# A graph layer's edge loop: who makes the turned selection matrix

## The chip, the cores and the metric

One Trainium2 chip, of which the kernel uses one core. The time is that of one execution on the device, in microseconds (us), as the median of several runs. A core has five engines that run their own instruction streams: PE (matrix multiply), DVE (vector), ACT (scalar, activations), POOL (GpSimd) and SP (DMA issue and semaphores). They meet by semaphores alone. Small differences, of about 0.3% (13 us here), can't be told from no change.

## The reference, cut to what matters

The layer works on N = 6250 nodes of 256 features and on E = 200000 edges (`src`, `dst`, sorted by `dst`). It adds a graph attention layer and a global polynomial attention ("mix"), and then a mixture of 16 experts. The change is in the edge part:

```python
xw = (x @ W).reshape(N, H, C)                 # H = 8 heads of C = 32
e = leaky_relu(a_src[src] + a_dst[dst], 0.2)  # one logit per edge and head
ex = exp(e - m[dst])
denom = segment_sum(ex, dst)
out = segment_sum(xw[src] * ex, dst) / denom  # then bias and relu
```

## The kernel before

The program goes through stages one after the other: setup and projections (to about 600 us of the profile), the edge loop (about 600 to 3510 us), routing (to about 3760 us), experts (to about 4220 us) and the last norm. Only the edge loop and two small allocations are touched.

The edge loop has 392 chunks of 512 edges (four tiles of 128). The edges are sorted by destination, and destinations lie in 49 blocks of 128 nodes, so a chunk on the border of two blocks is worked on twice: 440 steps, each with one chunk and one block. Over the first 208 steps the loop also computes the mix attention for 13 groups of 512 queries, one group in 16 steps (`query`, with k = 0 to 15 saying which pieces come in which step); the last 224 steps have edge work only. Here is who does what in step s:

- POOL gathers the 128 rows of each tile from `node_rows` by an indirect DMA (L923), four for a chunk, into a ring of R = 4 chunks (`rows_g`). Before it refills a slot it waits for `msg_ready`, that is, until DVE has finished (L1112) with the last step that needed the old chunk. SP counts the chunks that have landed (L940) and fetches the next indices (L936).
- ACT loads `dst_all[s+4]`, the chunk's destinations broadcast over 128 partitions (L962), computes `exp` of the logits into `msg` (L1010), and squares the mix features (L975), whose matmuls wait for it.
- DVE makes the two selections for step s+1. `sel_t` (L1030) has a node of the block in each partition and an edge in each column, and is 1 where the edge's destination is the node. It is made as `is_equal` of `dst_all` and the partition's number `iota_col`, in bf16. `sel` (L1036) has edges in the partitions and nodes in the columns, in fp32. Then it waits for the chunk (L1097) and for the spread values (L1098), and computes the logits (L1102, L1104, L1106), the block's sum of step s-2 (`accumulate`, L1045), a piece of the mix, and, after ACT's exp, the weighted rows (L1112).
- PE multiplies `sel_t` with the block's attention terms (`spread`, L1134, twelve small matmuls), which gives each edge its destination's terms; it waits for the logits of step s before it spreads for s+1. It multiplies `sel` with `msg` (`aggregate`, L1143, eight records). In the step order of PE, aggregate(s-1) comes first, then the mix pieces of the step, then spread(s+1).

There are two buffers of `sel_t`, so the one of step s may be overwritten when spread(s-2) is done (`dst_spread`). Four PSUM banks serve the mix pieces in turn, so that every fifth matmul waits until ACT or DVE has emptied the bank used four pieces earlier (`bank_free`, L885). `load_dst` in ACT's body waits for `sel_t_ready` of step s (L1011), because the loaded buffer is the one that `sel_t` of step s was made from.

Of the kernel before, what the change touches and what calls it, by code (L numbers as in the profile page):

```python
# [123 lines left out]
def gps_layer(nc, x, src, dst, gnn_W, att_src, att_dst, gnn_bias, Wqkv, bqkv, Wproj, bproj, temperature,  # L124
# [12 lines left out]
    with top:  # L137
# [14 lines left out]
        iota_col = sb("iota_col", [P, 1])  # L152
        ones = sb("ones", [P, P])
# [31 lines left out]
        blk_row = sb("blk_row", [1, SP_], I32, ctx=early)  # L185
        need_row = sb("need_row", [1, SP_], I32, ctx=early)
        first_row = sb("first_row", [1, CHUNKS], I32, ctx=early)
# [13 lines left out]
        with ExitStack() as c:  # L201
# [104 lines left out]
            def _(dve):  # L306
# [11 lines left out]
                dve.tensor_copy(iota_col[:], iota_ci[:])  # L318
                dve.wait_ge(ident_ready, 1)
# [352 lines left out]
        with ExitStack() as c:  # L672
# [58 lines left out]
            def _(dve):  # L731
# [21 lines left out]
                dve.tensor_copy(first_row[:], fdf[:])  # L753
# [21 lines left out]
                dve.tensor_scalar(blk_row[:], p_b[0:1, :], float(T - 1), None, ALU.min)  # L775
                dve.tensor_copy(need_row[:], p_need[0:1, :])
# [37 lines left out]
        with ExitStack() as c:  # L814
            idx = [sb(f"idx{i}", [P, TC], I32, ctx=c) for i in range(R)]
            rows_g = sb("rows_g", [P, R, TC, ROW], ctx=c)
            msg = [sb(f"msg{i}", [P, TC, ROW], ctx=c) for i in range(2)]
            dst_all = [sb(f"dst_all{i}", [P, TC * P], BF16, ctx=c) for i in range(R)]
# [136 lines left out]
            def _(act):  # L955
# [7 lines left out]

                def take_queries(n, g):
                    act.wait_ge(act_filled, act_count(n, f"T{g}"))
                    act.copy(q_t[g][:], bank(f"T{g}")[:]).then_inc(act_freed, 1)
# [39 lines left out]
                def body(s, k, n, last):  # L1006
                    j = k % R
                    wait(act, msg_summed, s - 1)
                    act.wait_ge(logit_ready, s + 1)
                    act.activation(msg[j % 2][:, :, D:ROW], lg[j % 2][:], ACT.Exp).then_inc(weight_ready, 1)  # L1010
                    act.wait_ge(sel_t_ready, s + 1)  # L1011
                    load_dst(s + R, j)
                    if n is not None:
                        query(n, k)

                load(0)
                for j in range(R):
                    load_dst(j, j)
                rounds(act, body)
# [5 lines left out]
            def _(dve):  # L1025
                def select_turned(s, j):

                    dve.wait_ge(dst_in[j], (s - j) * (16 // R) + 16)
                    wait(dve, dst_spread, s - 1)
                    dve.tensor_scalar(sel_t[j % 2][:], dst_all[j][:], iota_col[:], None, ALU.is_equal).then_inc(sel_t_ready, 1)  # L1030

# [56 lines left out]
                def body(s, k, n, last):  # L1088
# [6 lines left out]
                    select_turned(s + 1, j1)  # L1095
# [18 lines left out]
                select_turned(0, 0)  # L1114
# [731 lines left out]
```

## Time and profile before

| what | us |
|---|---|
| median of three runs | 4401.64 |
| lowest and highest | 4396.38, 4409.33 |
| the profiled execution, whole | 4418.26 |
| its span, first to last instruction | 4416.5 |

The profile is one execution. A row of its fifth part or of the view of groups names line, engine, operation and tiles, the count, the busy time and mean duration in ns of one, and then the idle time of the engine just before them with what ended it. In a timeline row the first number is the start, the second the duration, and the bracket tells how long the engine had been idle and who released it. A releaser is inferred; "issue" means that the profile shows nothing that was waited for, and "remote" that the release came from something that it can't name.

### The profile page before, as it was taken

The numbers are of one execution on the slowest core, as the hardware profiler recorded it, in microseconds if no ns is written. First come the engines' busy times: TensorE is split into PE (matmuls) and PEld (weight loads), VectorE is DVE, ScalarE is ACT, GpSimd is POOL, SyncE is SP. The second block draws the span as 40 slices with busy tenths as digits, with TensorE's granted clock in tenths as the row PEclk, the third lists the DMA queues.
The fourth block names the chain that finished last, engine by engine and source line by source line (L and its number), as shares of the span: only waits on it lengthen the run. The fifth ranks groups of instructions, "written<-read, shape, count | busy, mean of one in ns | idle before, by whom it ended". The sixth has DMA issues, their size and how long they took to land. (4 is left out here: it accounts for less than half of the span.)

```text
span 4416.5 us, 65073 instructions
## 1 busy us (share of the span) xinstructions
PE 2861.2 (65%) x15683; PEld 1908.1 (43%) x15684; DVE 2359.4 (53%) x5089; ACT 649.8 (15%) x1729; POOL 2272.4 (51%) x2161
## 2 busy tenths in 40 slices
PE   5888747777777777777554555555545542899940
PEld 2444324444444444444343333334334341788830
DVE  6888755544555554555554545545545674211137
ACT  2333212211221222222000000000000000122210
POOL 3777635554555555555566656656566555000035
PEclk9999868877878888888777777777777655999975
DMA  3000033333333333333333333433333312777743
GB/s 117 29 29 27 22 82 92 93 93 86 90 92 91 94 91 88 93 91 91 99 100 99 100 99 99 104 99 101 98 98 103 83 47 108 225 232 232 232 126 117
DMA packets 335340, 451.54 MB, mean 102 GB/s; under 512 B 113998, under 2 KB 247660, under 8 KB 335190
## 3 DMA queue, kind: packets, MB, share of 16 engines
q0 software_dynamic: 91088, 256.16, 21.0%
q1 hardware_dynamic: 172806, 128.68, 9.9%
q10 hardware_dynamic: 71328, 65.57, 5.5%
q14 instruction: 97, 0.79, 0.1%
q8 instruction: 21, 0.34, 0.0%
HBM read 395.09 MB, written 56.69 MB: 102 GB/s over the span
## 5 line engine op out<-in xcount | busy, mean ns | idle before, releaser
L923 POOL DMA_INDIRECT rows_g<-node_rows,idx x1568 | 1655.2, 1056 | 1284.2 <-DVE msg L1112 776.8
L1143 PE MATMUL p_m<-msg,sel 128*128 128x264 f32 x3520 | 1185.9, 491 | 255.1 <-DVE msg L1112 140.6
L1143 PEld LDWEIGHTS p_m<-msg,sel 128*128 128x128 f32 x3520 | 805.2, 241 | 438.7 <-issue 286.6
L1102 DVE TENSOR_TENSOR lg<-rows_g,p_m 128x32 f32<-128x32 f32 x440 | 81.5, 185 | 1116.0 <-remote 735.9
L1134 PE MATMUL p_m<-adm_parts,sel_t 128*128 x5292 | 247.0, 173 | 587.6 <-DVE lg L1106 469.9
L1134 PEld LDWEIGHTS p_m<-adm_parts,sel_t 128*128 128x128 bf16 x5292 | 216.1, 100 | 833.1 <-issue 808.3
L1112 DVE TENSOR_TENSOR msg<-rows_g,msg 128x1024 f32<-128x1024 f32 x440 | 540.7, 1229 | 24.2 <-ACT msg L1010 5.9
L1010 ACT ACTIVATE msg<-lg 128x32 f32<-128x32 f32 x440 | 101.2, 230 | 2001.2 <-DVE lg L1106 1476.3
L1036 DVE TENSOR_TENSOR sel<-iota_bf,dst_t 128x512 f32<-128x512 bf16 x441 | 301.0, 683 | 0.1
L975 ACT ACTIVATE qfeat<-p_scr 128x512 f32<-128x512 f32 x442 | 235.0, 601 | 440.1 <-remote 199.7
L1728 POOL DMA_DIRECT2D slot_y<-ysb x64 | 34.6, 541 | 472.9 <-DVE ysb L1718 472.9
L1030 DVE TENSOR_SCALAR sel_t<-dst_all,iota_col 128x512 bf16<-128x512 bf16 x441 | 168.3, 382 | 190.1 <-issue 175.8
L401 DVE TENSOR_TENSOR acc<-kk 128x512 f32<-128x512 f32 x250 | 251.3, 1037 | 0.1
L1671 PE MATMUL e_ph<-xst,wa 128*128 128x256 f32 x1024 | 234.1, 382 | 4.0 <-DMA bb<-in_L_ffn_b_dram 3.1
L1680 PE MATMUL e_py<-wb,ht 128*128 128x256 f32 x1024 | 231.4, 379 | 0.0
L1160 PE MATMUL p_scr<-q_t,sel_sum 32*128 32x512 f32 x832 | 187.7, 721 | 39.6 <-ACT qfeat L975 16.8
L401 POOL TENSOR_TENSOR acc<-kk 128x512 f32<-128x512 f32 x150 | 213.3, 1448 | 0.0
L1671 PEld LDWEIGHTS e_ph<-xst,wa 128*128 128x128 f32 x1024 | 196.1, 192 | 31.6 <-DMA bb<-in_L_ffn_b_dram 3.5
L1680 PEld LDWEIGHTS e_py<-wb,ht 128*128 128x128 f32 x1024 | 189.7, 190 | 23.2
L1045 DVE TENSOR_TENSOR acc<-acc,p_m 128x264 f32 x440 | 188.9, 429 | 4.4 <-PE p_m L1134 1.5
L1701 ACT ACTIVATE ht<-e_ph,ba 128x256 f32<-128x256 f32 x256 | 100.3, 474 | 422.5 <-PE e_ph L1671 422.5
L1710 DVE COPY xst<-e_px 128x512 f32<-128x512 f32 x64 | 44.3, 692 | 212.1 <-PE e_px L1661 212.1
(307 smaller groups left out, 3046.7 us busy)
## 6 DMA issues: line engine op xcount, KB each, us to landing
dst_all<-dst_bc ACTq DMA_DIRECT2D x444, 128.0 KB
wa<-in_L_ffn_w_dram SPq DMA_DIRECT2D x64, 512.0 KB, 3.9
wb<-in_L_ffn_w_dram SPq DMA_DIRECT2D x64, 512.0 KB, 5.2
rows_g<-node_rows,idx POOLq DMA_INDIRECT x1568
xs<-slot_x SPq DMA_DIRECT2D x64, 256.0 KB, 3.2
slot_y<-ysb POOLq DMA_DIRECT2D x64, 256.0 KB, 4.4
bb<-in_L_ffn_b_dram SPq DMA_DIRECT2D x64, 128.0 KB, 5.2
qs<-qn_dram ACTq DMA_DIRECT2D x14, 512.0 KB
```

The costliest lines, as they stand in the source:

```text
L401: return eng.tensor_tensor(feat.rearrange("p (d i) -> p d i", i=C), bass.AP(base.tensor, base.offset, [whole, [0, DIAGS - 1], [1, C]]), ba ...
L923: pool.indirect_dma_start(rows_g[:, j, u, :], None, node_rows, bass.IndirectOffsetOnAxis(ap=idx[j][:, u:u + 1], axis=0)).then_inc(gathered ...
L975: act.activation(feat[slot(name)][:], bank(name)[:], ACT.Square).then_inc(act_freed, 1)
L1030: dve.tensor_scalar(sel_t[j % 2][:], dst_all[j][:], iota_col[:], None, ALU.is_equal).then_inc(sel_t_ready, 1)
L1036: dve.tensor_tensor(sel[j][:], iota_bf[:].unsqueeze(1).broadcast_to([P, TC, P]), d.unsqueeze(2).broadcast_to([P, TC, P]), ALU.is_equal).th ...
L1045: dve.tensor_tensor(a, a, p_m[j % 2][:, 0:ROW], ALU.add).then_inc(acc_added, 1)
L1112: dve.tensor_tensor(m4, g3[:, :, 0:D].rearrange("p u (h e) -> p u h e", h=H), msg[j % 2][:, :, D:ROW].unsqueeze(3).broadcast_to([P, TC, H, ...
L1134: mm = pe.matmul(p_e(j)[:, u * 2 * H:(u + 1) * 2 * H], sel_t[j % 2][:, u * P:(u + 1) * P], adm_parts[:, bass.ds(b, 1), part, :].rearrange( ...
L1143: mm = pe.matmul(p_m[j % 2][:, 0:ROW], sel[j][:, u, :], msg[j % 2][:, u, :], start=(u == 0), stop=(u == TC - 1))
L1160: pe.matmul(bank(name)[:], sel_sum[rows, m * P:(m + 1) * P], q_t[g][rows, :], start=True, stop=True).then_inc(act_filled, 1)
L1671: mm = pe.matmul(p_h[s % 2][:, m * SLOT_ROWS:(m + 1) * SLOT_ROWS], wa[s][:, k, m * P:(m + 1) * P], xst[s % 2][:, k, :], start=(k == 0), st ...
L1680: mm = pe.matmul(p_y[s % 2][:, a * D:(a + 1) * D], ht[s % 2][:, k, a * P:(a + 1) * P], wb[s][:, k, :], start=(k == 0), stop=(k == KF - 1))
```

## The change

The turned selection `sel_t` is made by ACT in place of DVE. ACT takes the square of `dst_all - partition number` into a new bf16 tile `apart`, and then `relu(1 - apart)`, which is 1 where the difference is zero and 0 where it is another whole number. It does so for step s+2 in step s, after its exp and its load, ahead of the squares of the mix. The wait for `sel_t_ready` in ACT goes. DVE keeps `sel`. To find room for `apart`, three one-row tables share one tile (rows 0, 32 and 64 of it), which changes where they are read from and nothing else. One [128, 1] operation in the setup makes the negated partition number.

```diff
@@ setup
+        iota_neg = sb("iota_neg", [P, 1])
-        blk_row = sb("blk_row", [1, SP_], I32, ctx=early)
-        need_row = sb("need_row", [1, SP_], I32, ctx=early)
-        first_row = sb("first_row", [1, CHUNKS], I32, ctx=early)
+        tables = sb("tables", [2 * C + 1, SP_], I32, ctx=early)
+        blk_row = tables[0:1, :]
+        need_row = tables[C:C + 1, :]
+        first_row = tables[2 * C:2 * C + 1, 0:CHUNKS]
+                dve.tensor_scalar(iota_neg[:], iota_ci[:], -1.0, None, ALU.mult)
@@ edge loop
+            apart = [sb(f"apart{i}", [P, TC * P], BF16, ctx=c) for i in range(2)]
@@ scalar
+                def select_turned(s, j):
+
+                    act.wait_ge(dst_in[j], (s - j) * (16 // R) + 16)
+                    act.activation(apart[j % 2][:], dst_all[j][:], ACT.Square, bias=iota_neg[:])
+                    act.drain()
+                    wait(act, dst_spread, s - 1)
+                    act.activation(sel_t[j % 2][:], apart[j % 2][:], ACT.Relu, bias=ones[:, 0:1], scale=-1.0).then_inc(sel_t_ready, 1)
@@ scalar, body
                     act.activation(msg[j % 2][:, :, D:ROW], lg[j % 2][:], ACT.Exp).then_inc(weight_ready, 1)
-                    act.wait_ge(sel_t_ready, s + 1)
                     load_dst(s + R, j)
+                    select_turned(s + 2, (j + 2) % R)
                     if n is not None:
                         query(n, k)
@@ scalar, before the loop
+                for j in range(2):
+                    select_turned(j, j)
@@ vector
-                def select_turned(s, j):
-
-                    dve.wait_ge(dst_in[j], (s - j) * (16 // R) + 16)
-                    wait(dve, dst_spread, s - 1)
-                    dve.tensor_scalar(sel_t[j % 2][:], dst_all[j][:], iota_col[:], None, ALU.is_equal).then_inc(sel_t_ready, 1)
@@ vector, body
-                    select_turned(s + 1, j1)
                     select(s + 1, j1)
@@ vector, before the loop
-                select_turned(0, 0)
```

## Rows read from the trace of the kernel before

**Rows 1.** The page: each engine's busy time, share of the span, and count.
```profile
PE 2861.2 (65%) x15683; PEld 1908.1 (43%) x15684; DVE 2359.4 (53%) x5089; ACT 649.8 (15%) x1729; POOL 2272.4 (51%) x2161
```
**Rows 2.** Windows, edge loop with and without mix: busy (count) PE PEld DVE ACT POOL, clock.
```profile
604.00:2152.00 1548.00, 1153.15 (x6560) 651.98 (x6560) 811.28 (x1642) 315.03 (x711) 802.83 (x778) 0.82 0.35 92
2152.00:3515.00 1363.00, 734.23 (x4468) 539.67 (x4468) 704.08 (x1565) 51.44 (x224) 846.62 (x785) 0.73 0.38 100
```
**Rows 3.** Waits: engine and line, releaser, total us, times, longest.
```profile
POOL rows_g L923 <- DVE msg L1112: 776.8, 134, 11.8
...
DVE lg L1102 <- remote: 735.9, 135, 17.9
...
DVE lg L1102 <- SPq L940: 212.0, 30, 9.3
```
**Rows 4.** The page's groups, the gather and DVE's big operations in the edge loop.
```profile
L923 POOL DMA_INDIRECT rows_g<-node_rows,idx x1568 | 1655.2, 1056 | 1284.2 <-DVE msg L1112 776.8
...
L1036 DVE TENSOR_TENSOR sel<-iota_bf,dst_t 128x512 f32<-128x512 bf16 x441 | 301.0, 683 | 0.1
...
L1030 DVE TENSOR_SCALAR sel_t<-dst_all,iota_col 128x512 bf16<-128x512 bf16 x441 | 168.3, 382 | 190.1 <-issue 175.8
```
**Rows 5.** Timeline from 2823 us, a burst without mix work.
```profile
2823.20 0.19 DVE L1102 TENSOR_TENSOR lg<-rows_g,p_m 128x32 f32<-128x32 f32 x1 [9.73 <-remote]
...
2824.37 1.22 DVE L1112 TENSOR_TENSOR msg<-rows_g,msg 128x1024 f32<-128x1024 f32 x1
2825.70 3.86 PE L1143 MATMUL p_m<-msg,sel 128*128 128x264 f32 x8 [0.86 <-DVE msg L1112]
...
2826.43 1.32 POOL L923 DMA_INDIRECT rows_g<-node_rows,idx  x1 [5.90 <-DVE msg L1112]
2826.85 0.18 DVE L1102 TENSOR_TENSOR lg<-rows_g,p_m 128x32 f32<-128x32 f32 x1
...
2831.17 0.19 DVE L1102 TENSOR_TENSOR lg<-rows_g,p_m 128x32 f32<-128x32 f32 x1 [0.21 <-issue]
```
**Rows 6.** Timeline of POOL: the gather that begins the next train.
```profile
2847.50 1.21 POOL L923 DMA_INDIRECT rows_g<-node_rows,idx  x1 [5.38 <-DVE msg L1112]
```
**Rows 7.** Timeline: first and last `sel_t` inside a gather pause, with the gather that ends it.
```profile
652.11 0.34 DVE L1030 TENSOR_SCALAR sel_t<-dst_all,iota_col 128x512 bf16<-128x512 bf16 x1
...
653.10 0.94 POOL L923 DMA_INDIRECT rows_g<-node_rows,idx  x1 [4.48 <-DVE msg L1112]
...
3478.77 0.35 DVE L1030 TENSOR_SCALAR sel_t<-dst_all,iota_col 128x512 bf16<-128x512 bf16 x1 [0.42 <-issue]
...
3479.24 1.29 POOL L923 DMA_INDIRECT rows_g<-node_rows,idx  x1 [4.51 <-DVE msg L1112]
```
**Rows 8.** Timeline of POOL: first and last gather that start while L1036 runs.
```profile
600.17 1.23 POOL L923 DMA_INDIRECT rows_g<-node_rows,idx  x1 [0.30 <-issue]
...
3500.72 1.23 POOL L923 DMA_INDIRECT rows_g<-node_rows,idx  x1 [0.30 <-issue]
```
**Rows 9.** Groups: ACT on 128x512, without and with a bias column; a table load.
```profile
L975 ACT ACTIVATE qfeat<-p_scr 128x512 f32<-128x512 f32 x442 | 235.0, 601 | 440.1 <-remote 199.7 <-PE p_scr L1160 117.7 <-PE p_scr L1173 68.9
...
L970 ACT ACTIVATE r_norm<-p_scr,c_col 128x512 f32<-128x512 f32 x26 | 18.1, 696 | 70.7 <-remote 47.7 <-PE p_scr L1188 22.6 <-issue 0.4
...
L1010 ACT ACT_TABLE_LOAD x1 | 1.3, 1283 | 60.7 <-issue 60.7
```
**Rows 10.** Timeline from 1224 us, a step with mix work (k = 4).
```profile
1224.88 0.23 ACT L1010 ACTIVATE msg<-lg 128x32 f32<-128x32 f32 x1 [3.76 <-DVE lg L1106]
...
1225.57 2.06 ACT L975 ACTIVATE qfeat<-p_scr 128x512 f32<-128x512 f32 x4 [0.46 <-issue]
...
1226.22 2.08 PE L1188 MATMUL p_scr<-q_gram,head_ones 128*128 128x512 f32 x2 [3.27 <-ACT qfeat L975]
...
1228.09 0.51 PE L1134 MATMUL p_m<-adm_parts,sel_t 128*128 x12
...
1230.29 0.18 DVE L1102 TENSOR_TENSOR lg<-rows_g,p_m 128x32 f32<-128x32 f32 x1
```

More of the change, by code:

```diff
@@ L752, in _ @@
                 dve.tensor_scalar(needcol[:], ccol[:], 1.0, None, ALU.add)
-                dve.tensor_copy(first_row[:], fdf[:])
+                dve.tensor_copy(first_row, fdf[:])
                 dve.drain()
@@ L774, in _ @@
                 dve.wait_ge(b_turned, 1)
-                dve.tensor_scalar(blk_row[:], p_b[0:1, :], float(T - 1), None, ALU.min)
-                dve.tensor_copy(need_row[:], p_need[0:1, :])
+                dve.tensor_scalar(blk_row, p_b[0:1, :], float(T - 1), None, ALU.min)
+                dve.tensor_copy(need_row, p_need[0:1, :])
                 for g in range(G4):
```

## The prediction

> **What bounds the kernel now.** I read the busy shares first [rows 1]: no engine is above 65%, ACT has 15%, so the bound has to be found by stage. The windows [rows 2] give the edge loop 2911 of 4416.5 us: 1548 with mix work and 1363 without. In the second, DVE is busy 704 us and POOL 847 of 1363. Neither is full, so the loop is a cycle of waits. The wait view shows its two halves [rows 3]: POOL waits for DVE's weighted rows 134 times, 776.8 us in all (5.8 us each), and DVE waits at its first logit operation, L1102, for something remote or for SP, 165 times, 947.9 us. They take turns. POOL fills the free slots in a train of gathers; DVE meanwhile is stopped before L1102 and goes on as the train ends. At 2823.20 it starts again after 9.73 us [rows 5], does three steps (L1102 at 2823.20, 2826.85 and 2831.17), and stops. Its first step frees a slot, and POOL, idle for 5.90 us, starts the next train at 2826.43; the train after that starts at 2847.50, again after 5.38 us of pause [rows 6]. So the period, 21.07 us here, is the train (15.69 us) plus the pause (5.38 us). Why DVE's wait lasts about as long as the train is not explained by these rows. The chunk that it needs had been gathered a ring earlier, and no wait is laid to ACT. I take it as a fact that making `sel_t` earlier does not touch.
>
> A saving counts, then, only if it is in the pause, shortens a train, or lets DVE do more steps before it stops.
>
> **The change, part by part.**
>
> *1. `sel_t` leaves DVE.* 441 operations, 168.3 us, 382 ns each [rows 4]. One step costs 3.65 us in the burst (2823.20 to 2826.85) [rows 5], so it would become 3.27. Where does it lie on the path? A pause that is ended by DVE's first step after the wait contains no `sel_t` before the release: L1102 at 2823.20, L1112 until 2825.59, POOL at 2826.43. There the saving is nil. But the chunk of the freed slot may span two steps, or the step is a long one of DVE's own; then a `sel_t` with its step stands inside the pause. I counted in the timeline all `sel_t` that run wholly while POOL pauses for over 1 us and are followed by `sel` and L1102 without a gap: 130, of which 56 are in the part without mix; the first is at 652.11, the last at 3478.77 [rows 7]. At 0.382 us the 56 give 21 us. Of the 74 in the mix part I count half, 14 us, since PE's signal to L1102 comes soon behind there. Together 35 us; the ends are 0 and 50.
>
> *2. Trains get shorter.* A gather is 1056 ns on average [rows 4]. By the timeline it is 945 ns where no DVE operation with two inputs in SBUF runs at its start (921 gathers). The 320 that start during L1112 take 1320 ns, and the 311 that start during L1036 take 1114 ns; the first and the last of these took 1.23 us [rows 8]. The pattern after L1112 is fixed: a gather held up by it ends 0.8 us later, the next comes 0.3 us behind, and falls into L1036, which stands behind `sel_t`. Without `sel_t`, L1036 begins 0.38 us earlier and is nearly over by then. The 311 hold 52 us of excess; I take half, 26 us, because other gathers will meet the moved L1036. Ends: 0 and 52.
>
> *3. The other 311 `sel_t`.* They run beside a train, or before a long wait of DVE: 311 x 0.382 = 119 us, hidden by the gathers. I take 0. If the cover fails, because the burst gets one more step done before it stops, the whole 119 can come back (rival A).
>
> *4. What ACT gets.* The trace has no square or relu on bf16 with a bias column. The nearest are the square without it, 601 ns, and L970 with a bias column on the same 128x512, 696 ns [rows 9]. I take 696 for each, as it has the column, and 0.2 us for the drain between them, the space that DVE's drains take between L1102 and L1106: 1.6 us per step, 441 x 1.6 = 706 us more of ACT, between 1.2 and 1.8 a step. Without mix work that is covered: exp (0.23) and this make 1.9 us in a step of at least 3.27. The waits added in front of it are for `dst_all[s+2]`, loaded two steps before (6.5 us at least), and for spread(s), which DVE's L1102 of this step had needed already; both are met. The load itself keeps its place. Behind them on ACT's queue stand the squares of the mix, and PE waits for those. At k = 4 [rows 10], exp starts at 1224.88, the squares at 1225.57, and PE's norm matmul, which needs a bank that the first square frees, at 1226.22; then come spread, until 1228.60, and L1102 at 1230.29. If the squares start 1.6 us later, spread ends at 1230.2 and L1102 starts with the usual 0.4 us behind it at 1230.6. In place of 0.38 us gained, 0.3 is lost. Such places, where a matmul needs a bank freed in the same step, are three in a group of 16 steps (the two gram matmuls and the second norm), 39 in all. The slack differs; between 0 and 1.2 us each, I take 0.5: 20 us lost. Ends 0 and 47.
>
> *5. The rest* (one setup operation on a [128, 1] tile, tables at other partitions, a wait less on ACT): nothing. Each is below 0.3 us or the same instruction as before. The activation tables are switched once on entering the loop (1283 ns, [rows 9]), and squares run beside exp with no switch there; relu is the new one.
>
> Sum: -35 - 26 + 20 = -41 us. The profiled execution took 4418.26 us, 16.6 above the median of 4401.64; it would become 4377, and the median 4361.
>
> *A page that speaks against it.* DVE's `is_equal` takes 382 ns where I price ACT's two activations at 1392 ns. The Trainium skill (ScalarE: Activation LUTs, Rules for kernel authors) says to do relu and the like on VectorE, as it is up to about three times as fast per element in bf16; these rows agree in direction. By that rule the move pays only while ACT is not waited for, which is what rival C is about.
>
> *A page that promises more.* Only 16 gathers start during a `sel_t`, and they take 981 ns, so the rows show little of a direct collision. The Trainium skill (SBUF — State Buffer, Who interferes with whom) says that a `tensor_scalar` in a two-port mode locks GpSimd out for its whole length, and that with two SBUF inputs DVE holds up GpSimd's reads. The second half fits the 1320 and 1114 ns. By the first half the trains would lose up to the 96 us in which the two overlap in the trace, and the median would come to about 4265; that belongs to rival A's end of the range.
>
> **The rivals.**
>
> *A. Longer trains.* If the burst fits a fourth step in before DVE stops, the same 392 chunks need fewer pauses. For it: after about one burst in four the third step already starts 3.6 and not 4.3 us after the second, and then a fourth often follows at once. Against it: in most bursts the third step waits for PE and not for DVE (4.32 us against 3.65), as aggregate alone takes 3.86 us there [rows 5]. If 134 pauses become 120, 14 x 5.8 = 81 us more go: 4361 - 81 = 4280.
>
> *B. Nothing.* The wait before L1102 ends with the train whatever DVE does, the steps in the pauses turn out to be bound by PE, and ACT's lateness eats the rest: 4400.
>
> *C. Slower: PE waits for ACT in the mix.* In 13 x 8 steps ACT has squares for PE. If each comes 1.6 us late on PE's path, 104 x 1.6 = 166 us are lost against 61 gained: 4507. It decides where PE's own work between the bank's fill and its next use (three matmuls, some 1.6 us) is shorter than ACT's delay. With a third of them it gives 4401.6 - 61 + 55, or 4396; with over half it is slower, about 4440.
>
> *D. It doesn't do what it says.* If relu needed another table than exp, two loads of 1.283 us would fall into each step, 1129 us; or ACT gets `dst_all` late and holds up exp. For it there is nothing in the trace.
>
> **How the numbers follow.** My forecast (4330 to 4388) has a chance of 0.44, A (4240 to 4330) 0.20, B (4388 to 4415) 0.18, C (above 4415) 0.16, D 0.02. The predicted time is 4361. The range 4260 to 4430 leaves out about half of C, D and the far end of A. Faster by more than 0.3% is below 4388: 0.44 + 0.20 and 0.01 of C, 0.65. Within 0.3%: 0.18. Slower: 0.17.
>
> **What would show it.** In the profile after, L1112 of one step to L1036 should be the distance that `sel_t` had, and the burst's step 3.27 us. Gathers should average 1.03 to 1.04 us, with fewer above 1.1 (step 2). POOL's pauses should stay near 134, and their sum fall from 777 by some 35 us (steps 1, 3); fewer than 125 pauses is rival A. ACT should show two new groups of 441 with 0.6 to 0.7 us each (step 4), and PE's waits for L975's squares grow by some 20 us; growth by over 100 us is rival C. The time in the window with mix should fall less than that without. What would make the prediction wrong most easily is the unexplained wait before L1102: if it hangs on a collision of `sel_t` with the gathers, it shrinks, and the time falls by far more than I say.

## The result, and the profile after

The changed kernel takes 4437.12 us (median of 20 runs, 4401.95 to 4457.02), the kernel before 4402.47 us (20 runs, 4365.3 to 4432.57). The ratio is 1.0078, with a 95% interval of 1.0060 to 1.0096: slower, where the prediction said 4361 and a range up to 4430. The profiled execution took 4457.02 us, 38.8 more than that of before (4418.26), and a little more than the medians differ (34.7).

The page of the changed kernel: spans, engines, and the groups that answer to [rows 1], [rows 4] and [rows 9] (busy us, mean ns | idle before, its releaser).

```profile
span 4455.4 us, 65520 instructions
...
PE 2877.5 (65%) x15683; PEld 1921.1 (43%) x15684; DVE 2236.3 (50%) x4649; ACT 1279.9 (29%) x2613; POOL 2241.3 (50%) x2161
...
L927 POOL DMA_INDIRECT rows_g<-node_rows,idx x1568 | 1624.1, 1036 | 1359.0 <-DVE msg L1119 850.0
...
L1044 DVE TENSOR_TENSOR sel<-iota_bf,dst_t 128x512 f32<-128x512 bf16 x441 | 304.8, 691 | 183.7 <-issue 172.4
L971 ACT ACTIVATE apart<-dst_all,iota_neg 128x512 bf16<-128x512 bf16 x442 | 320.2, 724 | 195.0 <-issue 132.7
L974 ACT ACTIVATE sel_t<-apart,ones 128x512 bf16<-128x512 bf16 x442 | 319.9, 724 | 30.5
```

The line numbers have moved: the gather is L927, the logits' first operation L1109 (L1102 before), the weighted rows L1119, spread L1140, aggregate L1149. DVE works 123.1 us less: `sel_t` took 168.3, but its records overlapped those of its neighbours for 45 of them. ACT works 630.1 us more, and a gather takes 1036 ns where it took 1056. So far it is what was asked for.

The same two stretches as in [rows 2], moved to the stages' new borders (start:end, us, then busy and count of PE, PEld, DVE, ACT, POOL, granted clock, DMA share, GB/s):

```profile
600.00:2160.00 1560.00, 1165.72 (x6561) 662.37 (x6562) 755.06 (x1426) 617.76 (x1145) 788.34 (x779) 0.82 0.36 91
2160.00:3547.00 1387.00, 733.64 (x4461) 541.53 (x4460) 636.35 (x1338) 374.35 (x670) 830.17 (x784) 0.72 0.39 98
```

Both stretches are longer (by 12 and 24 us) although DVE and POOL are busy for less in both. The part without mix work, in which ACT has nothing else to do, loses more. The waits say where the time went (engine and line, releaser, total us, times, longest). First the changed kernel, DVE's four rows and POOL's, beside [rows 3]:

```profile
DVE lg L1109 <- remote: 730.3, 133, 18.8
DVE lg L1109 <- SPq L944: 330.7, 50, 10.5
...
DVE lg L1109 <- PE p_m L1140: 144.9, 68, 9.8
DVE lg L1109 <- issue: 70.0, 42, 14.6
...
POOL rows_g L927 <- DVE msg L1119: 850.0, 150, 14.0
```

and the two rows of the kernel before that [rows 3] left out:

```profile
DVE lg L1102 <- PE p_m L1134: 122.8, 55, 17.5
DVE lg L1102 <- issue: 44.4, 26, 10.3
```

Before, DVE stood before its logits for 735.9 + 212.0 + 122.8 + 44.4 = 1115.1 us in 246 stops; after, for 1275.9 us in 293. That is 160.8 us more, against 123.1 us less work: a net of 37.7 us, and the span grew by 38.9. POOL's pauses follow: 150 in place of 134, 850.0 us in place of 776.8.

One of the stops, in the timeline of the changed kernel (start, duration, engine, line; in brackets the idle time before it and what ended it). DVE:

```profile
2453.50 0.19 DVE L1109 TENSOR_TENSOR lg<-rows_g,p_m 128x32 f32<-128x32 f32 x1 [0.48 <-remote]
...
2456.22 0.69 DVE L1044 TENSOR_TENSOR sel<-iota_bf,dst_t 128x512 f32<-128x512 bf16 x1 [0.37 <-issue]
2470.79 0.19 DVE L1109 TENSOR_TENSOR lg<-rows_g,p_m 128x32 f32<-128x32 f32 x1 [13.88 <-remote]
...
2474.12 0.18 DVE L1109 TENSOR_TENSOR lg<-rows_g,p_m 128x32 f32<-128x32 f32 x1
```

and PE and POOL beside it:

```profile
2454.45 0.66 PE L1140 MATMUL p_m<-adm_parts,sel_t 128*128 x12 [0.68 <-issue]
2455.95 2.02 PE L1149 MATMUL p_m<-msg,sel 128*128 128x264 f32 x8 [0.84 <-issue]
...
2466.98 0.95 POOL L927 DMA_INDIRECT rows_g<-node_rows,idx  x1 [0.30 <-issue]
2474.04 0.99 POOL L927 DMA_INDIRECT rows_g<-node_rows,idx  x1 [6.11 <-DVE msg L1119]
```

PE's records of spread for the next step stand at 2454.45 to 2455.11. DVE asks for it at 2456.91 and is let go only at 2470.79, after POOL's train ended at 2467.93. The view puts these stops down to something "remote", because the work named had long been recorded. DVE stands there at two semaphores, `chunks_in` (SP's) and `dst_spread` (PE's). The trace also holds records of the semaphores' updates: that of `chunks_in` stands at 2454.61, and that of `dst_spread` at 2470.43, which is 15.3 us after spread's last matmul record and 0.36 us before DVE goes on. So it is PE's signal that comes late.

I counted this for all stops of over 1 us before the logits. In the kernel before there are 201, and in 168 of them an update of `dst_spread` is recorded within 0.7 us before DVE goes on, 145 times more than 1 us after spread's last record (at most 19.6). In the changed kernel there are 240, and the numbers are 220 and 178. Stops with a fresh update of `chunks_in` alone stay at 10 and 11. (Part of the update records is missing in these traces, as the last section tells, so the counts are lower bounds.) So the stops that were added are on spread too, although the views give part of them to SP.

DVE's next step comes 3.33 us later (2474.12), so the shorter step of the prediction's step 1 is there. It is not used, because there are more stops.

### The profile page after: what moved, and what is told of

Its sections match the earlier page's. It is cut to its first block and busy times, and to the rows that moved or that the text cites. A ratio compares the mean times of both kernels' runs of the same rounds, so it can differ in the third digit from the quotient of the medians.

```text
span 4455.4 us, 65520 instructions
## 1 busy us (share of the span) xinstructions
PE 2877.5 (65%) x15683; PEld 1921.1 (43%) x15684; DVE 2236.3 (50%) x4649; ACT 1279.9 (29%) x2613; POOL 2241.3 (50%) x2161
## 5 line engine op out<-in xcount | busy, mean ns | idle before, releaser
L927 POOL DMA_INDIRECT rows_g<-node_rows,idx x1568 | 1624.1, 1036 | 1359.0 <-DVE msg L1119 850.0
L1149 PE MATMUL p_m<-msg,sel 128*128 128x264 f32 x3520 | 1215.3, 499 | 250.0 <-DVE msg L1119 138.8
L1149 PEld LDWEIGHTS p_m<-msg,sel 128*128 128x128 f32 x3520 | 821.9, 246 | 439.3 <-issue 281.0
L1109 DVE TENSOR_TENSOR lg<-rows_g,p_m 128x32 f32<-128x32 f32 x440 | 81.9, 186 | 1279.5 <-remote 730.3
L1140 PE MATMUL p_m<-adm_parts,sel_t 128*128 x5292 | 244.2, 173 | 617.2 <-DVE lg L1113 452.3
L1140 PEld LDWEIGHTS p_m<-adm_parts,sel_t 128*128 128x128 bf16 x5292 | 215.9, 100 | 864.7 <-issue 839.6
L1119 DVE TENSOR_TENSOR msg<-rows_g,msg 128x1024 f32<-128x1024 f32 x440 | 539.7, 1226 | 27.5 <-ACT msg L1022 11.0
L971 ACT ACTIVATE apart<-dst_all,iota_neg 128x512 bf16<-128x512 bf16 x442 | 320.2, 724 | 195.0 <-issue 132.7
L974 ACT ACTIVATE sel_t<-apart,ones 128x512 bf16<-128x512 bf16 x442 | 319.9, 724 | 30.5
L1166 PE MATMUL p_scr<-q_t,sel_sum 32*128 32x512 f32 x832 | 181.3, 728 | 36.5 <-ACT qfeat L987 16.2
```

Source lines behind the costliest of these rows:

```text
L927: pool.indirect_dma_start(rows_g[:, j, u, :], None, node_rows, bass.IndirectOffsetOnAxis(ap=idx[j][:, u:u + 1], axis=0)).then_inc(gathered ...
L971: act.activation(apart[j % 2][:], dst_all[j][:], ACT.Square, bias=iota_neg[:])
L974: act.activation(sel_t[j % 2][:], apart[j % 2][:], ACT.Relu, bias=ones[:, 0:1], scale=-1.0).then_inc(sel_t_ready, 1)
L1119: dve.tensor_tensor(m4, g3[:, :, 0:D].rearrange("p u (h e) -> p u h e", h=H), msg[j % 2][:, :, D:ROW].unsqueeze(3).broadcast_to([P, TC, H, ...
L1140: mm = pe.matmul(p_e(j)[:, u * 2 * H:(u + 1) * 2 * H], sel_t[j % 2][:, u * P:(u + 1) * P], adm_parts[:, bass.ds(b, 1), part, :].rearrange( ...
L1149: mm = pe.matmul(p_m[j % 2][:, 0:ROW], sel[j][:, u, :], msg[j % 2][:, u, :], start=(u == 0), stop=(u == TC - 1))
```

## The experiments

Every ratio below is to the kernel before, run on the same chip in the same study. The kernel before took 4379.78 us there for the e runs, 4302.86 for the f runs, 4386.44 for the g runs, 4315.47 for m2, and 3745.65 and 3742.75 for the h, k and m1 runs. That last jump is a finding of its own, taken up below. The edits are cut to their main lines, and `...` marks what is left out. Each profiled execution is one of a kernel's runs, on its own chip, so two profiles can differ by more or less than the medians do.

### Is it DVE's shorter stream, or ACT's new work?

**e1_no_sel_t.** The kernel before, with `sel_t` made by nobody in the loop: DVE is relieved as in the change. ACT gets no work, only a wait for a load of four steps ago in place of that for `sel_t`.

```diff
...
-                    select_turned(s + 1, j1)
                     select(s + 1, j1)
...
-                    pe.wait_ge(sel_t_ready, s + 1)
+                    pe.wait_ge(sel_t_ready, 2)
```

> Leaves out the turned selection in the loop: sel_t is made twice ahead of it and never again, by nobody; ACT is as in the kernel before. Theory A (what ACT was given costs the time, the relief of DVE is worth about what I forecast): 4340 to 4365, so 1 to 1.5% below before. Theory B (the relief of DVE itself costs, because a faster DVE stops sooner before L1102 and more pauses of POOL follow, as the trace after shows 182 pauses over 1 us and not 160): as slow as the changed kernel, 4420 to 4440. If both have a part it lies at 4400.

Measured: 4427.29 us, 1.0117 (1.0075 to 1.0158). Taking away 441 operations and giving nobody more work makes the kernel slower, by about as much as the change does (1.0078 and, in m2, 1.0134). DVE's stops at the logits:

```profile
DVE lg L1101 <- remote: 758.1, 133, 18.8
DVE lg L1101 <- SPq L940: 292.8, 47, 8.6
...
DVE lg L1101 <- PE p_m L1134: 144.9, 78, 8.3
DVE lg L1101 <- issue: 32.2, 28, 8.3
```

That is 1228.0 us in 286 stops, where the kernel before had 1115.1 in 246. The profiled execution was the shortest of the seven, 4386.01 us, and even it has the additional stops.

**e2_both.** The changed kernel, in which ACT does both activations for nothing and DVE makes `sel_t` as before.

```diff
-                    act.activation(sel_t[j % 2][:], apart[j % 2][:], ACT.Relu, bias=ones[:, 0:1], scale=-1.0).then_inc(sel_t_ready, 1)
+                    act.activation(apart[j % 2][:], apart[j % 2][:], ACT.Relu, bias=ones[:, 0:1], scale=-1.0)
...
+                    select_turned(s + 1, j1)
                     select(s + 1, j1)
```

> DVE makes sel_t as before, and ACT does the square and the relu as well, in the place where the change has them, but into its own tile, which nobody reads. Theory A: ACT's work alone costs; this kernel is 35 to 75 us slower than before (4437 to 4480). Theory B: ACT's work is covered; 4395 to 4410, within 0.3% of before.

Measured: 4394.34 us, 1.0024 (0.9993 to 1.0055). ACT's 1.45 us a step cost 0.2%, if anything. This prices ACT's load, not its delivery, since nobody waits here for what ACT makes. DVE's stops at the logits, in its waits:

```profile
DVE lg L1116 <- remote: 724.3, 133, 18.0
DVE lg L1116 <- SPq L944: 226.1, 35, 9.4
...
DVE lg L1116 <- PE p_m L1148: 97.7, 47, 19.4
DVE lg L1116 <- issue: 34.6, 24, 11.6
```

1082.7 us in 239 stops, as before (1115.1 in 246), with ACT as loaded as in the changed kernel. So the 47 stops more of the changed kernel did not come with ACT's load, and e1 has 40 more with no work on ACT at all.

**e3_after_squares.** The changed kernel with ACT's two activations behind the mix squares.

```diff
-                    select_turned(s + 2, (j + 2) % R)
                     if n is not None:
                         query(n, k)
+                    select_turned(s + 2, (j + 2) % R)
```

> The changed kernel with the two activations behind the squares of the mix in ACT's step and not ahead of them. Rival C of the prediction (PE waits for the squares that come late): it gains 20 to 50 us on the changed kernel, 4390 to 4415, all of it in the part with mix. Theory B: no change, 4430 to 4445, since the loss stands in the part without mix too.

Measured: 4449.81 us, 1.0154 (1.0111 to 1.0197). If PE had waited for late squares (rival C), this would have won back the loss. It did not. Whether it lost more than the change itself can't be told, since the changed kernel was not run on this chip, and it lost 0.8% on one chip and 1.3% on another.

### Is it really spread that DVE waits for?

**e4_no_spread.** The kernel before without spread's matmuls; the logits are made with a constant. The waits between PE and DVE that belong to spread go too.

```diff
...
-                    dve.wait_ge(dst_spread, s + 1)
...
-                    pe3 = p_e(j).rearrange("p (u a) -> p u a", u=TC)
+                    pe3 = ones[:, 0:TC * 2 * H].rearrange("p (u a) -> p u a", u=TC)
...
-                    spread(s + 1, j + 1, b)
```

> The kernel before without the spread matmuls (L1134); the logits read a constant instead, and DVE waits for chunks alone. It asks what the long waits before L1102 hang on. If they hang on the chunks' landing, they stay: about 1000 us of DVE's idle time before L1102 and a time above 4300. If they hang on PE's spread being reported late, they all but go: the loop is then bound by the gathers, 1568 x 1.25 to 1.36 us or some 2050 us in place of 2911, and the time is near 3550 to 3700. If PE is late as a whole, the wait moves to the accumulate (L1045), and the time is in between.

Measured: 4160.42 us, 0.9497 (0.9435 to 0.9559). Four groups of DVE on its page, and POOL's pauses among its waits:

```profile
L1110 DVE TENSOR_TENSOR msg<-rows_g,msg 128x1024 f32<-128x1024 f32 x440 | 540.3, 1228 | 243.8 <-ACT msg L1010 145.9
...
L1044 DVE TENSOR_TENSOR acc<-acc,p_m 128x264 f32 x440 | 188.8, 429 | 121.2 <-remote 69.4
...
L1029 DVE TENSOR_SCALAR sel_t<-dst_all,iota_col 128x512 bf16<-128x512 bf16 x441 | 157.9, 358 | 369.1 <-issue 313.2
...
L1100 DVE TENSOR_TENSOR lg<-rows_g,ones 128x32 f32<-128x32 f32 x440 | 81.9, 186 | 169.7 <-issue 108.6
...
POOL rows_g L923 <- DVE msg L1110: 479.0, 91, 12.0
```

DVE's idle time before the logits falls from over 1100 us to 169.7, and POOL's pauses from 134 to 91. SP's row at the logits, which could have meant late chunks, falls from 212.0 to 49.8 us. So the wait that the prediction left unexplained is for the most part the wait for spread's end. But only 219 us are won of the 945 that go there. More than half of it comes back as waits of DVE at other lines: 243.8 us before the weighted rows where it was 24.2, 369.1 before `sel_t` (190.1) and 121.2 before the block's sum (4.4). The time lies in between, as was expected for "PE is late as a whole", and DVE waits at the block's sum for something remote (69.4 us): spread's signal seems not to be the only late one.

### What makes spread's end late?

**f1_static_spread** and **f1a_static_spread_after.** A constant address in place of a register's, in either kernel.

```diff
-    adm_parts[:, bass.ds(b, 1), part, :].rearrange("p a f -> p (a f)"), start=(part == 0), stop=(part == 2))
+    adm_parts[:, 0:1, part, :].rearrange("p a f -> p (a f)"), start=(part == 0), stop=(part == 2))
```

> The kernel before, with the 12 spread matmuls of a tile reading adm_parts of block 0 always (a constant address) in place of the block's own (an address held in a register). What they compute for later blocks is therefore wrong; the number and the shape of the instructions stay. Theory 'the register address is what makes spread's end come late under the gathers': the stops of DVE before the first addition of the logits go as they went without spread (4160 us), so 4160 to 4230 us. Rival 'it is the matmuls' own number, or the reading of the event': 4370 to 4410 us, as the kernel before.

> The same edit on the changed kernel (spread reads block 0 always). If the stop before the logits goes with the register address, the change can show what it gains without that stop: below the run f1_static_spread by 10 to 60 us (0.3 to 1.5%). If the stop stays, it is above it by 0.6 to 1.2%, as the changed kernel is above the kernel before.

Measured: 4286.96 us, 0.9981 (0.9956 to 1.0006), and 4346.3 us, 1.0126 (1.0085 to 1.0166). The address doesn't matter, and the change costs 1.45% between these two (1.0126 / 0.9981), somewhat more than expected. These are also a kernel without the change and one with it, both profiled on one chip: DVE stands before its logits for 946.5 us in 250 stops in the first and 1170.7 us in 290 in the second, and POOL's pauses go from 598.0 us in 117 to 744.4 in 141. (The first profile is of the shortest of its runs, 4270.27 us.)

**f2_one_part.** One part of `adm` in place of three: 4 matmuls for a step in place of 12.

```diff
-                        for part in range(3):
+                        for part in range(1):
```

> The kernel before with one part of adm in place of three in spread (4 matmuls for a tile in place of 12; the sum lacks the two smaller parts). Theory 'each of spread's matmuls is held for a time of its own under the gathers': two thirds of what taking spread away gave (4380 to 4160) go, 4220 to 4280 us. Rival 'the end of spread is held once, whatever its number of matmuls': over 4350 us.

Measured: 4193.34 us, 0.9778 (0.9730 to 0.9826). The expected 4220 to 4280 stood on a kernel before of 4380, so it meant 0.9635 to 0.977: the gain is there, at its small end or just outside.

**f3_no_dst_all_loads.** Without the broadcast loads, the second largest user of the DMA engines in the loop.

```diff
-                    load_dst(s + R, j)
```

> The kernel before without the loads of dst_all in the loop (the broadcast of each tile's targets to 128 partitions is left out, so the turned selections are those of the first ones). Theory 'PE's late end is traffic on the DMA rings': over 50 us faster. Rival 'these loads stand beside it and hold nobody': within 0.3% of the kernel before.

Measured: 4348.57 us, 1.0125 (1.0084 to 1.0167). Neither theory has this. With less traffic, and `sel_t` down to 354 ns on DVE, the kernel is slower. Its stops at the logits sum up to 1083.8 us, beside 946.5 in f1_static_spread on the same chip, whose median is that of the kernel before (but whose profiled execution was its shortest). Again something is made easier and the stops grow; in which way is open.

**g3_width_120.** Spread's weight loads are the only ones of the kernel whose record has a pattern in four pieces. The Trainium skill (TensorE: Matmul & The Clock Gate, Weight-path perf modes) calls it the fast weight load and says it is on for 128 weights of a type that is not fp32. 120 columns turn it off.

```diff
-    sel_t[j % 2][:, u * P:(u + 1) * P],
+    sel_t[j % 2][:, u * P:u * P + 120],
...
```

> The kernel before, with spread's weights 120 columns wide in place of 128 (the last 8 targets of each tile get the zeros or the leftovers that stand in the bank, so their logits are wrong); the number and order of all instructions stay. In the kernel before the record of each of spread's weight loads names a pattern in four pieces of 32 columns; no other weight load of the kernel has it. Theory 'it is this fast form of the weight load that is held while the gathers write': with 120 columns the load is of the plain form and most of the stops before the logits go, ratio to the kernel before 0.94 to 0.97. Rival 'it is the number of matmuls, or where they stand': 0.995 to 1.005.

Measured: 4393.67 us, 1.0000 (0.9973 to 1.0027). The form did change, which agrees with that rule: the loads' median went from 96 to 135 ns, as this line's own view shows (duration ns min/median/max).

```profile
L1137 PEld LDWEIGHTS p_m<-adm_parts,sel_t x5292: 129/135/225, 594.9 to 3487.6; 128*120 128x120 bf16 x196
```

The mean of a load went from 100 to 163 ns, and from its first matmul record to its last, spread takes 0.96 us where it took 0.51. That is 0.44 us more in each step, and nothing is lost: neither the form nor the duration of spread sets the time.

**g4_spread_twice.** Every matmul of spread done twice, 24 for a step.

```diff
-                        for part in range(3):
+                        for part in (0, 1, 2, 0, 1, 2):
```

> The kernel before with every matmul of spread done twice (24 for a tile; the second three overwrite the first). Theory 'each weight load of this form is held for a time of its own': slower by as much as the 12 cost, 100 to 250 us (ratio 1.025 to 1.06). Rival 'the end of spread is held once': within 0.5% (12 more matmuls take 0.3 us of an engine that is mostly idle).

Measured: 4592.92 us, 1.0464 (1.0430 to 1.0498). Twelve matmuls more in each of 440 steps cost 206 us, 0.47 us a step. By their records they take 0.32 us (spread 0.83 in place of 0.51), on an engine that then waits; in g3 spread grew by 0.44 us with no more matmuls, and cost nothing. DVE's and POOL's waits:

```profile
DVE lg L1102 <- remote: 927.7, 175, 18.2
...
DVE lg L1102 <- SPq L940: 258.1, 35, 9.2
...
POOL rows_g L923 <- DVE msg L1112: 994.8, 177, 14.8
```

There are 175 remote stops where there were 135. With none, 4, 12 and 24 matmuls the ratio is 0.950, 0.978, 1 and 1.046 (each beside the kernel before on its own chip; e4 lost some waits between engines as well). It goes by their number, not by their form, their address or their length.

**g2_fp32** and **g2a_fp32_after.** `sel_t` and `adm` in fp32, so that spread is 4 fp32 matmuls, before and after.

```diff
...
-                        for part in range(3):
-                            mm = pe.matmul(p_e(j)[:, u * 2 * H:(u + 1) * 2 * H], sel_t[j % 2][:, u * P:(u + 1) * P],
-                                           adm_parts[:, bass.ds(b, 1), part, :].rearrange("p a f -> p (a f)"), start=(part == 0), stop=(part == 2))
+                        mm = pe.matmul(p_e(j)[:, u * 2 * H:(u + 1) * 2 * H], sel_t[j % 2][:, u * P:(u + 1) * P],
+                                       adm[:, bass.ds(b, 1), :].rearrange("p a f -> p (a f)"), start=True, stop=True)
```

> The kernel before with sel_t and adm in fp32: spread is 4 matmuls for a tile in place of 12, none of them with the load in four pieces; DVE writes sel_t in fp32. Fast-load theory: the stops go as in the run without spread, less what a longer sel_t costs DVE in the quick steps: ratio 0.94 to 0.98. Rival 'number of matmuls': no better than one part in place of three, 0.975 to 1.0.

> The same edit on the changed kernel: sel_t is written in fp32 by ACT and spread is 4 fp32 matmuls. If the loss of the change lies in the stops that a shorter DVE stream runs into, it is gone with them, and taking sel_t from DVE is a gain: 10 to 60 us below g2_fp32, and the fastest of all correct versions. If ACT's two activations or their order cost something of their own, it is above g2_fp32 by 0.5 to 1.2%.

Measured: 4361.46 us, 0.9943 (0.9919 to 0.9967), and 4390.67 us, 1.0017 (0.9995 to 1.0038). The first gains less than one part did. The traces show why that need not speak against the number of matmuls: PE's records count 3528 in fp32, two for each matmul of the program, so a step has 8 where it had 12 (5292) and one part had 4 (1764). The ratio 0.994 lies between those of 12 and 4. `sel_t` in fp32 also takes DVE 509 ns in place of 382, and the two were not separated. The second misses what was expected: with two thirds of spread's records the change still loses, by 0.7% (1.0017 / 0.9943).

### Another chip, and the change without the stops

**h1_pe_idle_waits.** Twelve waits on a count long reached, behind spread, on PE's sequencer.

```diff
                     mm.then_inc(dst_spread, 1)
+                    for _ in range(12):
+                        pe.wait_ge(sel_t_ready, 1)
```

> The kernel before with 12 more instructions of PE's sequencer for a tile, right behind spread: waits on a count that was reached long ago, with no matmul. Theory 'PE is held by the supply of its instructions, whatever they are': slower by half of what 12 more matmuls with their weight loads cost (1.046), so 1.015 to 1.03. Rival 'it is matmuls and their ends that are held': 0.997 to 1.004.

Measured: 3778.79 us, 1.0086 (1.0072 to 1.0100), between the two. But this study ran on a chip on which the kernel before takes 3745.65 us, so it doesn't answer the question about the long stops, which aren't there. In this trace no stop before the logits is remote and none is longer than 4.6 us (before: 17.9), and of the 49 over 1 us with a fresh update of `dst_spread` none has it later than 0.02 us after spread's last record.

**h2_no_spread_after.** The changed kernel without spread, the same edit as in e4.

```diff
...
-                    spread(s + 1, j + 1, b)
```

> The changed kernel without spread (the logits are made with a constant in place of what spread brings, and nothing waits for it). Its partner is e4_no_spread, the kernel before with the same left out (0.9497 of the kernel before). Theory 'the change loses by the stops on spread that a shorter DVE stream runs into': without spread those stops are gone, so the change gains what step 1 and 2 of the prediction said: 0.935 to 0.948. Rival 'ACT's added work, or the order on ACT, costs by itself': 0.955 to 0.965.

Measured: 3680.68 us, 0.9829 (0.9815 to 0.9842). Its partner e4 ran on a chip of the other kind, so neither expectation can be read off. What it does say: on this chip all of spread and the change together are worth 1.7%, where spread alone was worth 5% on the other. No pause of POOL behind DVE is left in this trace. Without spread the two kinds of chip still stand at 3681 and 4160 us, so the late signal of spread is only part of what sets them apart.

**k1_wide_spread** and **k1a_wide_after.** The three parts side by side in one matmul of 48 columns, so 4 matmuls for a step, and one DVE operation more that adds the parts; before and after.

```diff
...
+                        mm = pe.matmul(p_e(j)[:, u * 6 * H:(u + 1) * 6 * H], sel_t[j % 2][:, u * P:(u + 1) * P],
+                                       adm_parts[:, bass.ds(b, 1), :, :].rearrange("p a q f -> p (a q f)"), start=True, stop=True)
...
+                    pe3 = adm_sum[j % 2][:]
+                    dve.tensor_reduce(pe3, p_e(j).rearrange("p (u q a) -> p u a q", u=TC, q=3), AXX, ALU.add)
+                    dve.drain()
```

> The kernel before, with the three parts of adm side by side in one matmul of 48 columns (4 matmuls for a tile in place of 12) and one more DVE operation for a tile, a sum over the parts, ahead of the logits. If it is spread's number of matmuls that sets how long the stops are, most of what one part gave (0.978) comes, less what 0.3 us more of DVE in a quick step costs (nothing up to 1.5%): 0.975 to 0.995. If it was the missing parts' work on something else, 1.0 to 1.02.

> The same edit on the changed kernel: ACT makes sel_t, DVE sums the parts, so that DVE's stream is about as long as in the kernel before. Theory 'the change loses by making DVE's stream shorter': here the 0.3 us are put back, and it comes out at k1_wide_spread within 0.4% of the kernel before. Rival 'ACT's work costs': above it by 0.6 to 1.2%.

Measured: 3736.79 us, 0.9976 (0.9966 to 0.9987), and 3683.01 us, 0.9841 (0.9828 to 0.9855). The second is not "within 0.4%" of the first: with ACT making `sel_t` it is 1.35% faster (0.9841 / 0.9976). On this chip the change gains in its wide form. Spans, gathers and POOL's pauses, first of k1:

```profile
span 3743.1 us, 58015 instructions
...
L924 POOL DMA_INDIRECT rows_g<-node_rows,idx x1568 | 1700.1, 1084 | 604.8 <-issue 473.6
...
POOL rows_g L924 <- DVE msg L1115: 98.6, 35, 8.8
```

then of k1a:

```profile
span 3678.4 us, 58462 instructions
...
L928 POOL DMA_INDIRECT rows_g<-node_rows,idx x1568 | 1593.8, 1016 | 650.8 <-issue 468.6
...
POOL rows_g L928 <- DVE msg L1122: 149.9, 47, 8.7
```

POOL pauses behind DVE for only 98.6 and 149.9 us in all: it is the bound here. The gathers take 106.3 us less, the pauses give back 51.3, and the sum, 55 us, is most of the 64.7 by which the span is shorter. About a third of the 106.3 is step 2 of the prediction: the gathers that start during `sel` fall from 357 to 46, and their excess over 945 ns from 42 to 7 us. The rest is something that the prediction didn't have: 389 gathers still start during the weighted rows (403 before), but they take 1213 ns in place of 1377, which is 70 us.

**m1_wide_after_again** and **m2_after_again** were meant to cross the kernels and the kinds of chip; each fell on the kind that had been seen.

> The kernel of k1a_wide_after once more. The kernel before took 4303 to 4402 us on the chips of the first three studies and 3746 us on that of the fourth, where the stops on spread were nearly absent. On a chip of the first kind, theory 'spread's number of matmuls sets the stops, and DVE's stream is back to its length': 0.975 to 0.99 of the kernel before. Rival 'the gain of k1a stood on the fast chip alone, since there the gathers bound the kernel': 1.0 to 1.01. On a chip of the second kind: 0.983 to 0.986 again.

> The changed kernel itself once more. On a chip where the kernel before takes 4300 to 4402 us: 1.005 to 1.013, as before. On one where it takes some 3745 us and hardly stops on spread, theory 'the loss is the stops on spread': the change gains what the prediction's steps 1 and 2 said and what the wide version gained beside its partner (0.9841 against 0.9976), so 0.980 to 0.995. Rival 'ACT's work, or its order, costs on any chip': 1.003 to 1.012 there too.

Measured: m1 3689.6 us, 0.9847 (0.9824 to 0.9869), where the kernel before takes 3742.75; m2, the changed kernel itself, 4367.52 us, 1.0134 (1.0102 to 1.0166), where it takes 4315.47. So both earlier results stand, and the crossing stays open.

## Why the prediction was wrong, point by point

The step that failed is step 3, with the sentence that it rests on. Steps 1, 2 and 4 are told first.

**Step 1** (35 us, `sel_t` out of the pauses). The shorter step came: 3.33 us in the stop shown, 3.27 predicted, 3.65 before. The gain did not come: POOL's pauses grew by 73.2 us where they should have fallen by some 35. The term was also a little large, as DVE's work fell by 123.1 us and not by 168.3, so one `sel_t` less is worth 0.28 us of DVE's time and not 0.382.

**Step 2** (26 us, shorter trains). Right: 1056 to 1036 ns, 31.1 us. So is its mechanism. In the trace after, 156 gathers start during `sel` where 311 did, and their excess over 945 ns is 17 us in place of 53; the excess of those that start during the weighted rows stays (123 and 120 us).

**Step 3** (the other `sel_t`, hidden, 0). Here the sum went wrong. The prediction said that the wait before L1102 was not explained and took it "as a fact" that the change doesn't touch. The change does touch it: 160.8 us more of waiting against 123.1 us less work (224.2 us more between f1 and f1a, on one chip). It is a wait for a late signal of PE's spread, and a shorter DVE stream meets it more often. The prediction priced a failing cover as a gain only, up to 119 us, and gave no price to a wait that grows. e1 shows this alone (+1.2% with no work added), e2 shows it vanish when DVE gets its operation back.

**Step 4** (ACT, 20 us lost, 1.6 us a step). The activations take 724 ns each where 696 was taken, and the idle time before the second is 30.5 us in all, 0.07 a step, where 0.2 was taken; together about 1.5 us. PE's matmuls waited for ACT's squares for 78.2 us before (rows of 39.6, 21.8 and 16.8) and 88.4 after (42.2, 28.5, 16.2 and 1.5): 10 us. e2 puts the price of ACT's load at 0.2%, at most 0.55%. In the changed kernel PE waits for ACT's `sel_t` once, for 8.1 us.

**Step 5.** Nothing was seen of it, and no run tried it by itself.

**The rivals.** A (longer trains, fewer pauses): the opposite, 150 pauses for 134. B: its first half, that the wait ends with the train whatever DVE does, was nearly the mechanism; it lacked that there would be more of them. C had the right side of zero by the wrong reason: PE's waits for squares grew by 10 us and not by over 100, and e2 and e3 speak against it. D: there are six table loads in either kernel, and the one wait of ACT for `dst_all` (61.9 us) stands at the loop's start. The sentence on what would make the prediction wrong most easily named the right wait and, again, only the direction in which it shrinks.

**What is shown and what isn't.** Shown: the stops are on spread's signal (the semaphore records, and e4); their cost goes with the number of spread's matmuls (e4, f2, g4, and g2 by its records) and not with address or length (f1, g3); less work on DVE, ACT left out, brings more of them (e1; f1 and f1a; e2 and the changed kernel side by side). Not shown: why a DVE that asks some 0.3 us earlier is caught more often. I counted in the traces the steps of the part without mix whose spread ended 1 to 2 us after the gathers' packets had begun again (behind a break of at least 1 us), and those among them with a stop of over 1 us: 13 of 53 before, 12 of 48 in e2, but 32 of 43 in the changed kernel and 32 of 39 in e1. Of the steps whose spread ended in such a break few stopped, 5 of 69 before and 1 of 83 after. The counts move with the limits chosen, but the contrast stays. That places the additional stops; it doesn't explain them. Nor is it shown that the changed kernel gains on a chip without the stops: only its wide version ran there.

## What to carry to other kernels

A wait that lasts as long as another engine's train, and that nobody's work explains, is not a constant of the kernel. Find what it hangs on first (leave the producer out for one run, as in e4), and give its growth a price too, before you sum up savings in front of it. Where stops like these stand, instructions saved on the engine whose signal comes late (f2: a third of the matmuls, 2.2%) are worth more than time saved on the engine that waits. One version is faster than the kernel before where it was run, k1a: ACT makes `sel_t`, and spread is one wide matmul for each of a chunk's four tiles. It takes 0.984 and 0.985 of that kernel's time, on the quicker chips alone; nothing is known of it on the others, and nothing of the changed kernel itself on the quicker ones.

## What the runs showed of the hardware

The same kernel took 4303 to 4402 us on some chips and 3743 to 3746 on others. The difference is in the edge loop. From the first of the logits' operations to the last it takes 2905 us in the kernel before, and 2298 in h1, the same kernel with twelve idle waits a step on a quicker chip; all that lies outside takes 1512 and 1474 us. The granted clock does not account for it: it is 0.82 and 0.93 in the part with mix, but 0.73 and 0.74 in the part without, and that part takes 1363 and 1125 us. The gathers are no shorter in themselves (945 to 948 ns undisturbed on either).

On the slower chips the records of some sequencers' own instructions are torn in the edge loop (a sequencer is the part of an engine that waits, branches and issues). The view of SP's line that ends its loop, of the kernel before (duration ns min/median/max):

```profile
L947 SPq FUSED_REGOPS  x96: 3/59/722, 620.0 to 3452.2; - x96
L947 SPq ALU_OP  x96: 3/37/1283, 651.4 to 3477.1; - x96
L947 SPq COMPARE_BRANCH  x96: 2/45/1426, 651.5 to 3477.2; - x96
```

and of k1_wide_spread, on a quicker one:

```profile
L948 SPq FUSED_REGOPS  x96: 59/59/69, 619.7 to 2827.5; - x96
L948 SPq ALU_OP  x96: 37/37/40, 640.9 to 2848.5; - x96
L948 SPq COMPARE_BRANCH  x96: 40/45/55, 641.0 to 2848.5; - x96
```

An instruction of 45 ns took up to 1426, and others "took" 2 or 3 ns, as if their records were written late and close together. Records of semaphore updates are missing as well: 148 are left of SP's 392 for `chunks_in`, where h1 has 390. POOL's and DVE's sequencers show the same torn records; PE's and ACT's don't (loading the block's number on PE's weight queue takes 296 to 322 ns in the loop here, and 296 to 318 in h1). Together with a cost that goes by the number of matmuls and not by their length, this suggests that what is held is the path by which instructions are reported or supplied. No run here tells these apart, and that PE's own records are whole while its signal is late is not explained. In particular, each execution shown was one that left such records, so whether the stops would stand without them is open. The Trainium skill (NOTIFIC — the notification-queue block, Overflow: three behaviours, one of which stalls the engine) says that this block's internal pipeline holds its producers back rather than lose a record; that would fit a late signal, less well the missing records, and no run here tests it.

A gather that starts during the weighted rows (L1112, two inputs in SBUF) took 1320 ns in the kernel before, 1379 in the changed kernel, 1437 in h1 and 1213 in k1a, against 945 to 948 where DVE does nothing of the kind. That part of the prediction held in every trace looked at.
